# A deformable convolution on one core: hats spread by TensorE and squared, in place of products and transposes, with the offset convolution in 16 tiles

## The reference, cut to what matters

```
offset = conv3x3(x, w_off) + b_off           # 18 numbers a pixel: dy, dx of 9 taps
y  = base_y + dy ;  xc = base_x + dx          # where tap k of pixel (i, j) looks
y0 = floor(y) ; x0 = floor(xc) ; wy = y - y0 ; wx = xc - x0
v  = v00*(1-wy)*(1-wx) + v01*(1-wy)*wx + v10*wy*(1-wx) + v11*wy*wx    # 0 outside
out = einsum('bckhw,ock->bohw', v, w_dcn)
```

## Time and profile before

| | us |
|---|---|
| median of 3 runs | 366.07 (363.42 to 366.41) |
| span of the profiled execution | 362.3 |
| PE busy | 305.1 (84%) |
| DVE busy | 199.4 (55%) |
| ACT busy | 158.0 (44%) |
| POOL busy | 46.7 (13%) |

### The profile page before, as it was taken

One profiled execution on the slowest core, in us unless ns is written; L12 is line 12 of the kernel. 1 busy time (PEld: TensorE's weight loads), 2 busy tenths in 40 slices (PEclk: granted clock), 3 DMA queues, 4 the chain that ended last, 5 costly groups with the idle time before them and its releaser, 6 DMA issues.

```text
span 362.3 us, 6423 instructions
## 1 busy us (share of the span) xinstructions
PE 305.1 (84%) x1972; PEld 198.7 (55%) x1972; DVE 199.4 (55%) x475; ACT 158.0 (44%) x337; POOL 46.7 (13%) x55
## 2 busy tenths in 40 slices
PE   8999699999886989988999788887897777697774
PEld 3665477776442458987996346576542443224521
DVE  4668868881067575788766564412522393225820
ACT  1196467765172256464570340121015285243950
POOL 4300811113000050005200000232000000000001
PEclk9999989999997999999999985989998999969999
DMA  2944100000000000000000000000000000000000
GB/s 77 240 101 107 50 0 0 0 0 0 2 0 0 0 4 0 2 0 1 0 2 0 1 2 0 2 0 0 0 18 7 13 0 0 16 16 0 0 0 29
DMA packets 4040, 6.23 MB, mean 17 GB/s; under 512 B 1170, under 2 KB 3602, under 8 KB 3733
## 3 DMA queue, kind: packets, MB, share of 16 engines
q1 hardware_dynamic: 3758, 5.70, 6.6%
q10 hardware_dynamic: 264, 0.30, 0.3%
HBM read 5.74 MB, written 0.26 MB: 17 GB/s over the span
## 4 chain that ended last, share of the span: by engine, by line
PE 58%; DVE 16%; ACT 9%; issue 7%; DMA 4%; POOL 2%; SPq 2%; DVEq 1%; POOLq 0%
PE ps L546 9%; PE ps L489 5%; PE ps L555 5%; DMA recB<-rec_b 4%; PE ps L712 3%; PE ps L718 3%; PE ps L508 2%; POOL arena L404 2%; PE ps L847 2%; PE ps L700 2%; ACT arena L1183 2%; DVE rmax L1610 2%; PE ps L959 1%; PE ps L839 1%; ACT arena L1018 1%
## 5 line engine op out<-in xcount | busy, mean ns | idle before, releaser
L489 PE MATMUL ps<-xC,cstb 128*128 128x512 f32 x114 | 55.1, 630 | 0.0
L1301 DVE TENSOR_TENSOR arena<-arena 128x512 f32 x72 | 44.6, 686 | 12.6 <-PE ps L546 8.0
L1025 ACT ACTIVATE arena<-ps 128x512 f32<-128x512 f32 x72 | 37.8, 602 | 20.7 <-PE ps L546 20.6
L489 PEld LDWEIGHTS ps<-xC,cstb 128*128 128x128 f32 x114 | 22.5, 206 | 29.0 <-issue 28.8
L546 PE MATMUL ps<-cstb,arena 128*128 128x128 f32 x288 | 37.3, 282 | 0.7 <-DVE arena L1301 0.7
L546 PEld LDWEIGHTS ps<-cstb,arena 128*128 128x128 f32 x288 | 32.0, 143 | 9.8 <-DVE arena L1301 8.5
L555 PE MATMUL ps<-arena 128*32 128x256 f32 x288 | 19.9, 396 | 3.5 <-POOL arena L404 3.4
L404 POOL COPY arena<-arena 128x256 f32 x18 | 15.4, 860 | 57.6 <-PE ps L555 44.6
L712 PE MATMUL ps<-arena 128*128 128x160 f32 x96 | 15.3, 307 | 2.5 <-issue 1.2
L1183 ACT ACTIVATE arena<-ps,rmax 128x256 f32<-128x256 f32 x32 | 14.8, 470 | 5.2 <-DVE rmax L1610 5.2
L458 POOL TENSOR_TENSOR arena<-w32b,cstb 128x1024 f32<-128x1024 f32 x4 | 7.6, 1893 | 63.8 <-PEq L833 49.6
(11 more groups left out here) (375 smaller groups left out, 548.7 us busy)
## 6 DMA issues: line engine op xcount, KB each, us to landing
toepb<-toep SPq DMA_DIRECT2D x1, 1536.0 KB
w32b<-w SPq DMA_DIRECT2D x1, 1225.0 KB
cstb<-cst SPq DMA_DIRECT2D x1, 1044.0 KB
recA<-rec_a SPq DMA_DIRECT2D x4, 128.5 KB
w1b<-moe_w SPq DMA_DIRECT2D x1, 264.0 KB
xC<-x SPq DMA_DIRECT2D x1, 256.0 KB, 2.8
w2b<-moe_w SPq DMA_DIRECT2D x1, 256.0 KB
out<-ln_a SPq DMA_DIRECT2D x1, 256.0 KB, 2.2
```

The lines of the kernel that those rows point to most:

```text
L489: mm(ps[7], ident if lhs is None else lhs, xC if rhs is None else rhs, start=True, stop=True)
L1025: af(SQ[:, c].rearrange("p q n -> p (q n)"), ps[c % BI], ACT.Copy).then_inc(S["s_ev"], 1)
L1301: tt_(ST[:, c], hy.unsqueeze(3).to_broadcast([P, PT, 16, 16]), hx.unsqueeze(2).to_broadcast([P, PT, 16, 16]), ALU.mult).then_inc(S["prod"], 1)
```

## The change

The stage is rewritten; the layers behind it stay as they are, but for the numbers of the semaphores. Instead of the product a*b of the two hats it uses 2ab = (a+b)^2 - a^2 - b^2.

- The offset convolution becomes 36 matmuls of 32 rows x 32 columns of the array with 512 moving columns (`w_off`; row block `bi`, column block k % 4). The four partial sums are carried to SBUF (`parts4`) and added by four matmuls with `eye32` on top of a matmul of constants (`lineb`: pixel coordinates, tap offsets, bias).
- Hats are kept compact: 32 lines (16 of y, 16 of x) for each tap and image pair. Five tiles come first: PE selects (`select`), ACT takes the distance (`distance`), DVE cuts it to a hat (`hat`). The four for taps 4 to 7 follow as item 10.
- An item is one `expand`: four matmuls, each with 32 rows of a constant matrix `spread` of zeros and ones as weights and one tap's 32 hat lines as 512 moving columns, in the four row blocks of the array and into four banks. What comes out is a+b for 128 pixels x 512. ACT squares three of the banks on the way out (`squares`), DVE copies the fourth and POOL squares the copy (`square_copy`). There are 18 such items; 5 and 6 carry the second half of the weight products, 10 the selection, 13 the sums of the weights (`GC`).
- `products(group, j)` are again 8 matmuls of 256 columns in column blocks; their weights are slices of `GS` (halved on the way out), with no staging. 18 such blocks, and 24 matmuls that take off the squares of the parts, end in `ps[7]`.
- Banks `ps[0]` to `ps[6]` go round, four for each item.
- The loops are written out. `lineb` and a 160 KB piece of constants (`mid_in`) come in ahead of `parb` and `rowb` on SP's queue; the first constants shrink from 92 to 22 KB, and the offset weights grow from 81 to 144 KB.

```diff
+GROUPS = {1: (1, 2, 3, 4), 2: (8, 9, 11, 12), 3: (14, 15, 16, 17), 4: (18, 19, 20, 21)}
+ITEM = {1: (0, 0, 0), 2: (0, 0, 1), 3: (0, 0, 2), 4: (0, 0, 3), 8: (0, 1, 0), 9: (0, 1, 1), 11: (0, 1, 2),
+        12: (0, 1, 3), 14: (1, 0, 0), 15: (1, 0, 1), 16: (1, 0, 2), 17: (1, 0, 3), 18: (1, 1, 0), 19: (1, 1, 1),
+        20: (1, 1, 2), 21: (1, 1, 3)}
+SQUARED = (0, 1, 2, 3, 4, 7, 8, 9, 11, 12, 14, 15, 16, 17, 18, 19, 20, 21)
+FREED = {8: 1, 9: 2, 11: 3, 12: 4, 14: 6, 15: 5, 16: 7, 17: 8, 18: 9, 19: 10, 20: 11, 21: 12}
+G_ITEM, SEL_ITEM, GC_ITEM = {5: 0, 6: 1}, 10, 13
+ALL_DCN = 18
...
-        GS = ar(0, 4608).rearrange("p (g t b k o) -> p g t b k o", g=BG, t=PT, b=BI, k=KK)
-        hat = ar(4608, 4608).rearrange("p (t b k a q) -> p t b k a q", t=PT, b=B, k=KK, a=2)
-        ST = ar(9216, 4096).rearrange("p (c t y x) -> p c t y x", c=B, t=PT, y=HH)
-        SQ = ar(13312, 4096).rearrange("p (c q n) -> p c q n", c=B, q=PT)
-        yx = ar(17408, 288).rearrange("p (t b o) -> p t b o", t=PT, b=B)
-        Gst = ar(17696, 512).rearrange("p (g t b o) -> p g t b o", g=BG, t=PT, b=BI)
+        GS = ar(0, 4608).rearrange("p (h b k o) -> p h b k o", h=PT, b=B, k=KK)
+        hats = [ar(4608 + 512 * i, 512) for i in range(9)]
+        hats2 = [ar(9216 + 512 * i, 512) for i in range(9)]
+        GC = ar(13824, 512).rearrange("p (b k o) -> p b k o", b=B, k=2)
...
+        parts4 = (ln_a, ln_b, lnC, tC)
...
+            sp.dma_start(lineb, lines).then_inc(S["par_in"], 16)
             sp.dma_start(cstb[:, 0:CST_EARLY], cst[:, 0:CST_EARLY]).then_inc(S["cst_in"], 16)
+            sp.dma_start(cstb[:, CST_EARLY:CST_MID], cst[:, CST_EARLY:CST_MID]).then_inc(S["mid_in"], 16)
             sp.dma_start(parb, par.unsqueeze(0).to_broadcast([B, CH, len(PAR)])).then_inc(S["par_in"], 16)
...
+            def square_copy(item):
+                pool.wait_ge(S["bank_dve"], DVE_FILL + item + 1)
+                v = home(item, 3)
+                nc.gpsimd.tensor_tensor(v, v, v, ALU.mult).then_inc(S["sq_pool"], 1)
+            for item in SQUARED[:5]:
+                square_copy(item)
+            for n in range(5):
+                pool.wait_ge(S["hat"], n + 1)
+                nc.gpsimd.tensor_tensor(hats2[n], hats[n], hats[n], ALU.mult).then_inc(S["hat_sq"], 1)
+            for item in SQUARED[5:]:
+                square_copy(item)
...
+            pe.wait_ge(S["par_in"], SMALL)
+            mm(ps[4], lineb[:, 0:P], lineb[:, P:LINES], start=True, stop=False, skip_group_check=True)
             pe.wait_ge(S["xn"], BG)
-            pe.wait_ge(S["pool_bd"], 1)
+            pe.wait_ge(S["w32_in"], 16)
+            w_off = w32_("off").rearrange("p (k o) -> p k o", k=KK)
+            for k in range(KK):
+                for bi in range(BI):
+                    rows, j = slice(32 * bi, 32 * bi + 32), k % 4
+                    last = mm(ps[bi][32 * j:32 * j + 32, :], w_off[rows, k, :],
+                              xnp[rows, :, k // 3:k // 3 + 16, k % 3:k % 3 + 16], start=(k < 4), stop=(k + 4 >= KK),
+                              skip_group_check=True)
+                    if k == KK - 1:
+                        last.then_inc(S["off_mm"], 1)
+            w_dcn = w32_("dcn")
+            def weight_products(half, g, bi, bank):
+                rows = slice(32 * bi, 32 * bi + 32)
+                mm(bank[:, 0:KK * C], xn[rows, g * N + half * P:g * N + half * P + P], w_dcn[rows, :],
+                   start=True, stop=True).then_inc(S["g_mm"], 1)
+            pe.wait_ge(S["taps_in"], 16)
+            pe.wait_ge(S["xn"], 2 * BG)
+            weight_products(0, 0, 0, ps[5])
+            weight_products(0, 0, 1, ps[6])
+            pe.wait_ge(S["bank_act"], FILL_ACT["part"])
+            weight_products(0, 0, 2, ps[0])
+            pe.wait_ge(S["bank_act"], FILL_ACT["part"] + 1)
+            weight_products(0, 0, 3, ps[1])
+            pe.wait_ge(S["bank_dve"], FILL_DVE["part"] + 1)
...
+            for bi in range(BI):
+                last = mm(ps[4][32 * bi:32 * bi + 32, :], eye32, parts4[bi], start=False, stop=True,
+                          skip_group_check=True)
+            last.then_inc(S["off_mm"], 1)
+            pe.wait_ge(S["bank_act"], FILL_ACT["sum"])
+            pe.wait_ge(S["pool_bd"], 2)
+            mm(ps[2], sel8_w, offC, start=True, stop=True
+               ).then_inc(S["sel_mm"], 1)
+            def select(kg, bi, bank):
+                rows = slice(32 * bi, 32 * bi + 32)
+                mm(bank, sel_w[rows, P * kg:P * kg + P], offC[rows, :],
+                   start=True, stop=True).then_inc(S["sel_mm"], 1)
+            pe.wait_ge(S["bank_act"], FILL_ACT["weights"] + 1)
+            for bi in range(BI):
+                select(0, bi, ps[3 + bi])
+            pe.wait_ge(S["bank_dve"], FILL_DVE["weights"])
+            weight_products(0, 1, 0, ps[0])
+            pe.wait_ge(S["bank_dve"], FILL_DVE["weights"] + 1)
+            weight_products(0, 1, 1, ps[1])
+            pe.wait_ge(S["bank_act"], FILL_ACT["far"])
+            weight_products(0, 1, 2, ps[2])
+            pe.wait_ge(S["bank_act"], FILL_ACT["far"] + 1)
+            weight_products(0, 1, 3, ps[3])
...
+            def expand(item):
+                kg, half, bi = ITEM[item]
+                if (item, bi) in ((1, 0), (2, 1), (3, 2), (4, 3)):
+                    pe.wait_ge(S["hat"], 2 + bi)
+                if kg:
+                    pe.wait_ge(S["hat"], 6 + bi)
+                for j in range(4):
+                    rows = slice(32 * j, 32 * j + 32)
+                    bank_free(item, j)
+                    last = mm(bank_of(item, j), spread[rows, half, :], hats[1 + 4 * kg + bi][rows, :],
+                              start=True, stop=True)
+                last.then_inc(S["ex_mm"], 1)
...
+            def products(group, j, stop=False):
+                kg, half, _ = ITEM[GROUPS[group][0]]
+                if j < 3:
+                    pe.wait_ge(S["bank_act"], ACT_FILL + 3 * GROUPS[group][3] + j + 1)
+                else:
+                    pe.wait_ge(S["sq_pool"], SQUARED.index(GROUPS[group][3]) + 1)
+                for g in range(BG):
+                    for bi in range(BI):
+                        last = onto(g, bi, GS[:, half, g * BI + bi, 4 * kg + j, :], home(GROUPS[group][bi], j), stop)
+                last.then_inc(S["dcn_mm"], 1)
...
+            expand8(0, 0)
+            pe.wait_ge(S["pool_zero"], 3)
+            mm(ps[7], zeros, xn, start=True, stop=False, skip_group_check=True)
+            expand(1)
+            expand(2)
+            products8(0, 0)
+            expand(3)
+            expand(4)
+            half_of_weights(5)
+            products(1, 0)
+            half_of_weights(6)
+            products(1, 1)
+            expand8(7, 1)
+            products(1, 2)
+            expand(8)
+            products(1, 3)
+            expand(9)
+            products8(7, 1)
+            for bi in range(BI):
+                bank_free(SEL_ITEM, bi)
+                select(1, bi, bank_of(SEL_ITEM, bi))
+            expand(11)
+            expand(12)
+            bank_free(GC_ITEM, 0)
...
+            for j in range(4):
+                expand(14 + j)
+                products(2, j)
+            for j in range(4):
+                expand(18 + j)
+                products(3, j)
+            pe.wait_ge(S["bank_act"], ACT_FILL + 3 * GC_ITEM + 3)
+            pe.wait_ge(S["bank_dve"], DVE_FILL + GC_ITEM + 1)
+            pe.wait_ge(S["hat_sq"], 5)
             for g in range(BG):
-                for k in range(KK):
-                    last = mm(ps[g][0:BI * NOFF, 0:N], off_bd[:, k, :, :], window(xnp, g, k // 3, k % 3, 16),
-                              start=(k == 0), stop=(k == KK - 1))
-                last.then_inc(S["off_mm"], 1)
...
-            pe.wait_ge(S["pool_bd"], 2)
-            pe.wait_ge(S["xn"], 2 * BG)
-            for r in range(BG * PT):
                 for bi in range(BI):
-                    if 0 < r <= PT:
-                        pe.wait_ge(S["g_ev"], (r - 1) * BI + bi + 1)
-                    elif r:
-                        pe.wait_ge(S["g_evD"], (r - 1 - PT) * BI + bi + 1)
-                    mm(ps[4 + bi][:, 0:KK * C], xn[:, r * P:r * P + P], dcn_bd[:, bi, :],
-                       start=True, stop=True).then_inc(S["g_mm"], 1)
-            pe.wait_ge(S["g_evD"], PT * BI)
-            pe.wait_ge(S["pool_zero"], 3)
+                    onto(g, bi, GC8[:, g, bi, :], hats2[0])
             for g in range(BG):
-                mm(ps[4 + g][:, 0:N], zeros, xn[:, 0:N], start=True, stop=False)
-            keep_busy(4)
-            pe.sem_inc(S["dcn_mm"], BG)
-            pe.sem_inc(S["tr"], B)
-            def transposes(k, g):
-                for c in range(g * BI, g * BI + BI):
-                    pe.wait_ge(S["prod"], k * B + c + 1)
-                    pe.wait_ge(S["s_ev"], k * B + c + 1)
-                    for q in range(PT):
-                        for t in range(PT):
```

(88 more changed lines are left out.)

315 lines of the change are left out of this document (198 added, 117 removed).

## The result

Four runs of the changed kernel beside four of the kernel before on the same chip: median 351.86 us (349.06 to 352.54) against 364.75 (362.14 to 366.41). The ratio is 0.9642, interval 0.9583 to 0.9701. The forecast was 346.3. The profiled span fell from 362.3 to 349.6, by 12.7 us where 19.8 were forecast.

A forecast was written before the change was run, and what follows sets the result against it. PE, busy 84% of the span, was taken as the bound, by transposes more than products. The stage's timetable ended at 68.4 for 88.15, 19.8 us less: 366.07 - 19.8 = 346.3 us, range 340 to 356.

The forecast's parts named there:

- The start: PE's first stage matmul waits for `par_in`: constants at 8.8 us, convolution starts at 9.7, 3 us later than before.
- the clock, which I had as a rival: Slow start: a wait to 10 drops PE to 1.2 GHz, 5.6 us more, 351.9; chance 0.13 together with the POOL rival.
- The offset convolution: The 36 small matmuls at the stage's start take 3.5 us, between 2.6 and 7.7, ending at 13.2.
- The fill: Uncovered chain from the convolution's end at 13.2 through partial sums, selection and distances to the end of item 0 at 21.5.
- The middle: Items 0 to 13: PE has 20.2 us of work and loses 3 us in waits, ending at 45.0.
- POOL was read rightly: POOL's 23 squares at 1.05 us need 24 of 45 us; nearest to late at about 37 us; no loss taken.
- The even part and the tail: Items 14 to 21, eight times 2.05 us, to 61.4; then 24 matmuls, 3.0, and four product blocks, 4.0, to 68.4.
- The bounds for it: Expansion takes 0.86 at least, 1.3 at most; over the sixteen PE sets, 2.5 us less or 4 more.
- Nothing is changed behind it: Behind the stage nothing changes: PE's `keep_busy` runs 2.77 us while DVE adds the residual, so only the last product's end counts.
- a table load: Rival: the layer behind is set by late loads or a table load; mostly given back, up to 366; chance 0.05.
- POOL becomes the bound: Rival: squares at 2.25 us, 23 take 52 us, last product at 76.5, 354.4; chance 0.13 together with the slow start.
- matmuls of 32 rows: Rival: waiting for banks, they do not run together; each expansion 3.4 us, time about 388; chance 0.03.

The follow-up runs named there:

- gap_filled: Changed kernel with two more matmuls of ones ahead of PE's wait for the small loads; median 351.67 us, ratio 0.9631 to the kernel before.
- lines_late: Changed kernel with the matmul of constants and its wait moved behind the first two weight products; median 349.45 us, ratio 0.9474 to the kernel before.
- conv_twice: lines_late with the 36 matmuls of the offset convolution run twice; the second pass cost 2.8 us, ratio 0.9565.
- pool_more: lines_late with POOL squaring each of its five hat tiles a second time; PE waits 3.62 us for item 7's square, stage ends some 5 us later.
- expand_twice: lines_late with the four spreading matmuls run twice in items 14 to 21; beat 2.93 us, stage ends 6.84 us later, span 350.6.
- table_early: Changed kernel with ACT's two waits before the Gelu in the other order; median 351.19 us, ratio 0.96.
- conv_columns: lines_late with the convolution's nine taps in another order, so matmuls of the same column block follow each other; convolution 5.1 us, ratio 0.9611.
- combined_again: The kernel of combined run once more, unchanged; median 347.42 us, ratio 0.9475 to the kernel before.
- combined_warm: combined with three added matmuls of ones, one before the wait for the sum and two within item 0; median 348.64 us, ratio 0.9513.
- combined: Changed kernel with the edits of lines_late and table_early together; median 347.63 us, ratio 0.9436 to the kernel before.

## Why the prediction was right, and where it was not

The direction, the mechanism and the range (340 to 356) held; the gain was 12.9 us between the medians where 19.8 were forecast. The time itself was 5.6 us above the forecast of 346.3 and not 6.9, by luck: the forecast started from a median of 366.07 for the kernel before, and beside the changed kernel that kernel took 364.75. In the profile 12.7 us: 13.8 in the stage (88.08 in the timeline to 74.28), less 1.3 behind it, and 0.2 elsewhere. Step by step against the kernel after:

- **The start.** The constants were forecast at 8.8 and begin at 8.99. The waiting itself was priced rightly. What the step left out of the sum was its second price, the clock, which I had as a rival with 5.6 us on conditions (a wait to 10) that were too strict: here the clock fell after 2.2 us of idle PE.
- **The offset convolution.** 4.65 us instead of 3.5; at full clock 3.14 (gap_filled, lines_late). The term was too high by 0.4 and the clock added 1.5. That sixteen tiles run together is shown by conv_twice.
- **The fill.** Forecast 8.3 us from the end of the convolution to the end of item 0, measured 9.2, and 9.0 at full clock (13.06 to 22.08). At full clock 0.2 of it are the way out of the four parts (their sum starts 1.5 behind the convolution and not 1.3), 0.2 the selection, and 0.4 the four distances, which end 2.6 after the selection and not 2.2.
- **The middle.** Forecast 23.5, measured 27.2, and 25.5 at full clock (22.08 to 47.59). This is the largest term that was mis-sized with no clock in it, by 2.0. PE's timeline of gap_filled shows where: the expansions of items 1 to 4 take 5.8 instead of 4.1 (two pairs, 2.91 and 2.84 from start to next start), the weight products of item 5 1.5 instead of 0.7, and the expansions of items 11 and 12, with 0.61 of waiting for ACT's distances, 4.2 instead of 2.1. That is 4.6 us of waits where 3 were put down. `GC` takes 2.1 instead of 1.7. Which of the waits would have to go first was not tried. (By its own terms, 20.2 and 3, the forecast would have ended at 44.7 and not 45.0.) POOL was read rightly as having no loss and little slack: pool_more found 1.4 us.
- **The even part and the tail.** 17.1 for 16.4, of which 0.6 are a first expansion held up by a bank that ACT still empties (1.76 for 1.14); 6.2 for 7.0, as blocks of products with no change between them take 0.86 and not 1.00. The beat of 2.07 for 2.05, with 0.17 for a change of blocks, is confirmed by expand_twice. (The bounds for it, 2.5 us less and 4 more, are 2.7 and 4.3 by their own values, 16 times 0.17 and 0.27.)
- **"Nothing is changed behind it".** This step was wrong by 1.3 us. I had looked only at `keep_busy` and the residual. The order of ACT's instructions after shows the wait for the convolution on the table load and not on the Gelu, and nothing of it was in the sum; table_early shows it to be the whole of the difference. In my rivals a table load stood as a word, with no price of its own.

Together: 3.3 us of the miss is the clock within the stage, 2.5 are the other terms of the stage (the middle 2.0, the fill, the even part and the start, less what the convolution and the tail gave back), 1.3 the table load. The rival "POOL becomes the bound" did not come about, as POOL's squares took 1.04, at most 1.42; matmuls of 32 rows do run together.

What stays open is why the rest differs from one execution to the next. In four kernels with the same instructions there it took 272.6 (after), 273.6 (gap_filled), 272.5 (conv_twice) and 270.7 us (conv_columns); with the two waits exchanged 272.2 (table_early), 274.2 (combined_again) and 273.5 (combined_warm); and 278.4 in lines_late and 276.5 in combined. The windows of gap_filled and conv_columns (columns as above), whose stages end within 0.7 us of each other, show where:

```profile
77.00:110.00 33.00, 24.77 (x82) 11.24 (x78) 17.62 (x50) 13.12 (x20) 0.00 (x0) 0.90 0.00 0
...
260.00:300.00 40.00, 32.14 (x167) 14.69 (x164) 17.71 (x45) 18.48 (x50) 0.00 (x0) 0.87 0.04 7
300.00:345.00 45.00, 32.09 (x183) 14.71 (x182) 18.88 (x53) 21.53 (x53) 1.27 (x1) 0.96 0.03 9
```

```profile
77.00:110.00 33.00, 24.76 (x88) 11.08 (x84) 17.62 (x50) 13.29 (x21) 0.00 (x0) 0.95 0.00 0
...
260.00:300.00 40.00, 29.06 (x173) 13.84 (x174) 18.23 (x49) 19.96 (x51) 0.00 (x0) 1.00 0.04 8
300.00:345.00 45.00, 33.09 (x182) 15.01 (x182) 18.35 (x49) 20.42 (x53) 1.26 (x1) 0.89 0.03 9
```

The granted clock differs between the two in the same stretches, though the instructions are the same: lower in two of them in the execution that takes longer, and higher in the last. A spread of 2 to 3 us in the rest is enough to hide the 3.5 us saved in gap_filled, or the 1.3 of table_early, in a ratio from four executions. What makes such a stretch fall in one execution and not in the next was not found.

## What to carry to other kernels

When a change opens a gap on PE where none was, price the gap twice: 2.2 us of waiting for a small load cost some 3 us of start and 1.5 to 1.7 us of clock, and moving one matmul and its wait behind the work that doesn't need it gave both back. The other 1.7 us of clock, lost behind the fill, came and went with and without the gap. Where the last instructions before a table load are rewritten, look in the order at which of two waits the load takes; writing two lines the other way round took 1.3 us out of the layer here, in the trace. And a filler belongs into a gap, not between matmuls of different row blocks, where it makes them run one after the other.

## What the runs showed of the hardware that I had not expected

- Matmuls of different column blocks overlap only as far as their order lets them: the same 36 took 3.14 us with neighbours in different column blocks and 5.1 with pairs in one.
- From 18 to 24 us, in the fill of the kernel after, PE was busy for 5.59 us, and the granted clock still was 0.50 from 24 to 27. The same loss stands in the second profile of that kernel and in those of conv_twice and conv_columns, but not in seven other profiles with the same instructions there (gap_filled, lines_late, pool_more, table_early, expand_twice, and both of combined).
- Squares on POOL took 1.04 us beside DVE's copies out of PSUM and 1.42 in the four cases in which DVE squared an SBUF tile at the time; neither is near the 8.0 us of the copy in the earlier trace rows.
